# Decoder of twelve layers on one core: first operands of eight layers loaded while the layer ahead runs, and another order in two layers

## The chip, the cores and the metric

One core of a Trainium2 chip runs the whole kernel as one launch. The metric is the device time in microseconds (us), the median of several runs; lower is better. The engines have short names in the profile: PE is TensorE, DVE is VectorE, ACT is ScalarE, POOL is GpSimd, SP is the engine that only issues transfers (DMA).

## The reference

A pre-norm decoder of depth 4, three layers each time, over x (8 batches of 256 tokens, width 128, float32) and a context of 8 x 512 rows of width 96. `_layernorm` is taken in front of each layer, and the result is added to x.

```python
x = x + L0_attn(_layernorm(x), ...)            # 0  gated recurrence
x = x + L0_xattn(_layernorm(x), ctx_768, ...)  # 1  cross attention, 16 heads of 8
x = x + L0_ffn(_layernorm(x), ...)             # 2  mixture: 64 experts, top 8, all computed
x = x + L1_attn(_layernorm(x), ...)            # 3  self attention, 16 heads of 8
x = x + L1_xattn(_layernorm(x), ctx_768, ...)  # 4  cross attention, one head
x = x + L1_ffn(_layernorm(x), ...)             # 5  FP4-quantised MLP
x = x + L2_attn(_layernorm(x), ...)            # 6  causal attention, 16 heads of 64
x = x + L2_xattn(_layernorm(x), ctx_768, ...)  # 7  cross attention, one head, inner norms
x = x + L2_ffn(_layernorm(x), ...)             # 8  shared expert, top-1 expert on 256 tokens
x = x + L3_attn(_layernorm(x), ...)            # 9  latent attention with rope
x = x + L3_xattn(_layernorm(x), ctx_768, ...)  # 10 cross attention, 16 heads of 8
x = x + L3_ffn(_layernorm(x), ...)             # 11 sign-quantised linear
```

The two layers whose inner order changes:

```python
# L0_ffn, xf = x as 2048 x 128, 64 experts of width 64
aff = xf @ centroids.T
_, idx = jax.lax.top_k(aff + expert_biases, 8)
w = jax.nn.sigmoid(take_along_axis(aff, idx)); w = w / (sum(w) + 1e-8)
cw = zeros((T, E)).at[arange(T)[:, None], idx].add(w)
h = silu(einsum('td,edf->etf', xf, W_up)); y = einsum('etf,efd->etd', h, W_down)
out = silu(xf @ Ws_up) @ Ws_down + einsum('etd,te->td', y, cw)

# L2_ffn, 256 tokens are picked by index_b, index_t
shared_out = _ln(silu(x1) * x2) @ sw3 + sb3
out_all    = _ln(silu(h1) * h2) @ ew3 + eb3          # per expert, picked tokens
final_out  = shared_out.at[index_b, index_t].set(shared_w * shared_out[...] + expert_w * expert_out)
```

## The kernel before

x stays in SBUF for the whole kernel. Each layer is one function with a block of five programs, one per engine, written out by hand; engines meet through semaphores. `allocators` gives a layer its tiles and semaphores, and its `clear` ends the layer with a barrier of all engines (L166). So nothing of a layer, its transfers included, starts before every engine is through with the layer ahead: the layer's own SP program issues all of its loads. The functions are `layer_attention_heads8` (layers 1, 3, 10), `layer_attention_single` (4, 7), `layer_fp4_mlp` (5), `layer_attention_heads64` (6, 9), `layer_moe_top8` (2) and `layer_selected_experts` (8).

**Layer 2** (`layer_moe_top8`, names `L_ffn_...` between 454 and 723 us of the span). 2048 tokens go in four groups g of 512. A group has 33 steps: step j=0 is the shared expert, the others are 32 pairs of experts. In step n TensorE does `up(n)` into `psU`, ScalarE `silu(n)` into one of 20 `act` tiles, VectorE `weigh(n)` (times the pair's weights, L2110), and TensorE, `LAG` = 17 steps later, `down(n)`, which gathers in `psY`. The pair's weights must stand on 128 partitions, 64 for each expert (e=0, e=1): the routing weights `cw` are turned by TensorE (`turn_weights`), copied by ScalarE (`copy_weights`, `cwT`), written to DRAM (`weights_by_expert`, L2036) and read back as a broadcast into `cwb`, a chunk of four pairs at a time, two transfers of 512 KB each (L2044), four chunks deep. The routing of group g+1 runs inside group g: on VectorE `route_a` (copy of the affinities `aff`, top 8) and `route_b`, on ScalarE `sigmoids` with a table load before and after. For group 0 and 1 the places are these:

```python
                if n == 10:
                    turn_weights(0)
                if g + 1 < NG:
                    if j == 12:
                        turn(g + 1)
                    if j == 14:
                        affinities(g + 1)
                    if j == 26:
                        turn_weights(g + 1)
```

and VectorE has `weigh(n)` first, then `route_a(g + 1)` at j == 16. ScalarE has `sigmoids(g + 1)` at j == 19.

**Layer 8** (`layer_selected_experts`, `L_ffn_...` between 1497 and 1560 us). For each batch b of 256 tokens the shared expert is `project(b)` (`psX`, L2614), a gated unit on ScalarE and VectorE (`uT`), `out(b)` (`psT`, L2634), layer-norm statistics by `out_moments(b)` on VectorE, a root on POOL (`orr`), and `take(b)` on VectorE, which adds to x. The 256 picked tokens have units SEL, BIAS and TURN of their own; their results come as `value`, are split into three bfloat16 parts (`part`) and are put in place by `scatter(b)` on TensorE (a bias matmul, L2706, and twelve products with a 0/1 matrix `spread`, L2712), and `add(b)` on VectorE. `project(6)` uses the bank that TURN's result was in, so it waits for `x_read`, which came with `rw` (L2551).

## Time and profile before

| what | us |
|---|---|
| median of 3 runs | 2268.08 (2263.37 to 2271.72) |
| profiled execution, its own time | 2276.47 |
| its span | 2274.7 |
| mean granted clock of TensorE | 0.909 |

The span is divided by the layers' starts at about 3.6 (layer 0), 106.3 (1), 454.4 (2), 723.4 (3), 919.0 (4), 980.7 (5), 1077.9 (6), 1423.8 (7), 1497.0 (8), 1560.2 (9), 1936.6 (10) and 2236 (11). A row of the timeline has the start, the duration, the engine and line, output and inputs, and in brackets how long the engine was idle ahead of it and what ended that. SPq and POOLq are the queues of an engine that issues transfers; PEld is TensorE's load of the stationary operand. The granted clock (PEclk) is 1.00 for 2.4 GHz and 0.50 for 1.2 GHz.

### The profile page before, as it was taken

How to read it: one execution, taken by the hardware profiler on the slowest of the kernel's cores; microseconds unless marked ns; L12 is line 12 of the kernel's file. 1: busy time of each engine (PE TensorE's matmuls, PEld its weight loads, DVE VectorE, ACT ScalarE, POOL GpSimd, SP SyncE). 2: the span in 40 equal slices, each digit the busy share in tenths (PEclk: the TensorE clock that was granted, in tenths of full speed). 3: DMA queues.
4: the chain of work that ended last, by engine and by line, in shares of the span. 5: the costliest groups of instructions: out<-in, count | busy, mean ns of one | idle time of the engine just before them, and what ended most of it. 6: DMA issues, size and time to landing. Idle time of an engine off the chain costs nothing. (4 is left out here: it accounts for less than half of the span.)

```text
span 2274.7 us, 37358 instructions
## 1 busy us (share of the span) xinstructions
PE 1980.8 (87%) x12479; PEld 1178.8 (52%) x12479; DVE 1396.7 (61%) x3165; ACT 1115.1 (49%) x2823; POOL 657.7 (29%) x940
## 2 busy tenths in 40 slices
PE   6769999969997788856999999887999999699987
PEld 3424454424443455534666676565666666244444
DVE  5458889644542665478666666674656665567762
ACT  4325555534331476333555554341666666267762
POOL 7443432100002441300111110733443332533312
PEclk8859999979998799878999999896999999599996
DMA  1043131098661431100000000101000000443321
GB/s 35 17 93 92 47 85 43 2 202 174 149 145 30 98 86 31 32 10 7 33 1 1 1 1 2 32 23 49 1 2 1 2 1 2 110 97 86 73 44 27
DMA packets 120861, 111.90 MB, mean 49 GB/s; under 512 B 55862, under 2 KB 93410, under 8 KB 118370
## 3 DMA queue, kind: packets, MB, share of 16 engines
q1 hardware_dynamic: 87394, 108.47, 20.4%
q10 hardware_dynamic: 33280, 1.05, 0.7%
q8 instruction: 103, 1.69, 0.3%
q14 instruction: 84, 0.69, 0.1%
HBM read 93.30 MB, written 15.20 MB: 48 GB/s over the span
## 5 line engine op out<-in xcount | busy, mean ns | idle before, releaser
L997 DVE TENSOR_REDUCE L_xattn_mx<-L_xattn_psS 128x1 f32<-128x512 f32 x512 | 326.5, 684 | 124.2 <-PE L_xattn_psS L1124 119.9
L1234 ACT ACTIVATE L_xattn_PT<-L_xattn_psT 128x512 f32<-128x512 f32 x512 | 283.2, 600 | 95.4 <-PE L_xattn_psT L1136 89.7
L627 ACT ACTIVATE L_attn_pr<-L_attn_psS,L_attn_negm 128x256 f32<-128x256 f32 (+1 forms) x512 | 222.5, 447 | 52.0 <-PE L_attn_psS L538 33.6
L1124 PE MATMUL L_xattn_psS<-L_xattn_KR,L_xattn_QR 72*128 72x512 bf16 x512 | 213.0, 421 | 39.4 <-DMA L_xattn_QR<-L_xattn_q_parts 23.2
L407 DVE TENSOR_REDUCE L_attn_negm<-L_attn_psS 128x2 f32<-128x512 f32 x256 | 165.0, 686 | 116.3 <-PE L_attn_psS L528 116.2
L1136 PE MATMUL L_xattn_psT<-L_xattn_QR,L_xattn_KR 75*128 75x256 bf16 x1024 | 198.1, 278 | 3.9 <-ACT L_xattn_PT L1234 1.6
L1150 PE MATMUL L_xattn_psO<-L_xattn_PT,L_xattn_V 128*32 128x256 f32 x2048 | 188.9, 390 | 3.2 <-ACT L_xattn_PT L1234 1.1
L2110 DVE TENSOR_TENSOR L_ffn_act<-L_ffn_act,L_ffn_cwb 128x512 f32<-128x512 f32 x128 | 86.7, 691 | 129.6 <-ACT L_ffn_act L2240 105.9
L528 PE MATMUL L_attn_psS<-L_attn_qk 64*128 64x256 f32 x1024 | 146.1, 403 | 8.7 <-ACT L_attn_pr L627 8.5
L2175 PE MATMUL L_ffn_psU<-L_ffn_hT,L_ffn_wup 128*128 128x512 f32 x256 | 133.2, 611 | 13.8 <-ACT L_ffn_act L2240 13.8
L2240 ACT ACTIVATE L_ffn_act<-L_ffn_psU 128x512 f32<-128x512 f32 (+1 forms) x132 | 78.5, 597 | 135.2 <-PE L_ffn_psU L2175 131.3
L332 POOL TENSOR_TENSOR L_attn_qk<-L_attn_rotc,L_attn_rots 128x512 f32<-128x512 f32 x64 | 81.1, 1267 | 210.2 <-DVE L_attn_rotc L395 163.6
L1136 PEld LDWEIGHTS L_xattn_psT<-L_xattn_QR,L_xattn_KR 75*128 75x128 bf16 x1024 | 100.3, 100 | 77.4 <-issue 12.1
L337 POOL COPY L_attn_rinv<-L_attn_inv 128x256 f32<-128x256 f32 x128 | 50.9, 398 | 285.5 <-DVE L_attn_inv L420 285.5
L1150 PEld LDWEIGHTS L_xattn_psO<-L_xattn_PT,L_xattn_V 128*32 128x32 f32 x2048 | 89.1, 111 | 79.7 <-issue 22.8
L2188 PE MATMUL L_ffn_psY<-L_ffn_act,L_ffn_wdn 128*128 128x512 f32 x256 | 129.4, 598 | 1.1 <-DVE L_ffn_act L2110 1.1
L563 PE MATMUL L_attn_psOR<-L_attn_prT,L_attn_V 128*64 128x256 f32 (+1 forms) x1024 | 125.3, 365 | 5.7 <-ACT L_attn_spread L640 5.7
L548 PE MATMUL L_attn_psT<-ident,L_attn_pr 128*128 128x128 f32 x896 | 121.3, 275 | 0.0
L1124 PEld LDWEIGHTS L_xattn_psS<-L_xattn_KR,L_xattn_QR 72*128 72x128 bf16 x512 | 51.9, 102 | 133.4 <-DVE L_xattn_mx L997 75.9
L548 PEld LDWEIGHTS L_attn_psT<-ident,L_attn_pr 128*128 128x128 f32 x896 | 100.3, 141 | 38.4 <-issue 31.9
L640 ACT COPY L_attn_spread<-L_attn_psOR 128x256 f32<-128x256 f32 x128 | 47.8, 373 | 139.1 <-PE L_attn_psOR L570 139.1
L999 DVE TENSOR_REDUCE L_attn_mx<-L_attn_psS 128x2 f32<-128x512 f32 x128 | 84.4, 687 | 48.4 <-PE L_attn_psS L1124 47.7
(593 smaller groups left out, 3912.8 us busy)
## 6 DMA issues: line engine op xcount, KB each, us to landing
L_ffn_cwb<-L_ffn_weights_by_expert SPq DMA_DIRECT2D x64, 512.0 KB, 13.1
...
```

The lines of the kernel that those rows point to most:

```text
L407: nc.vector.tensor_reduce(negm[:, n % 4, :, r], psS[g % 3][:], AX.X, ALU.max, negate=True).then_inc(negm_ready, 1)
L528: ins = nc.tensor.matmul(psS[g % 3][:, t], qk[b % 2][at, j, 0, t * P:(t + 1) * P], qk[b % 2][at, j, 1], start=(t == 0 or not causal), stop ...
L548: ins = nc.tensor.transpose(psT[r][:, at:at + P], pr[n % 3][:, r, t, k * P:(k + 1) * P], m.ident[:])
L563: ins = nc.tensor.matmul(psOR[r * DH:(r + 1) * DH, 0, first:S], V[b % 2][:, k, hd * DH:(hd + 1) * DH], prT[n % 2][:, r, k * S:k * S + widt ...
L627: ins = nc.scalar.activation(pr[n % 3][:, r, t, 0:width], psS[(2 * n + r) % 3][:, t, 0:width], ACT.Exp, bias=negm[:, n % 4, t, r:r + 1], a ...
L997: nc.vector.reduce_max(mx[:, b % 2, u, hd:hd + 1], psS[n % 2][:], AX.X).then_inc(s_used, 1)
L1124: ins = nc.tensor.matmul(psS[n % 2][:, i * keys:(i + 1) * keys], QR[b % NB][0:PAIR, hd, t * P:(t + 1) * P], KR[b % NB][0:PAIR, hd, :], sta ...
L1136: ins = nc.tensor.matmul(psT[n % NPS][:, k], KR[b % NB][0:ROWS, hd, kt * P:(kt + 1) * P], QR[b % NB][0:ROWS, hd, :], start=True, stop=True)
L1150: ins = nc.tensor.matmul(psO[r:r + HW, g % 2], V[b % NV][:, kt, n % H], PT[n % NPT][:, kt], start=(kt == 0), stop=(kt == NKT - 1))
L1234: nc.scalar.activation(PT[n % NPT][:, 2 * u:2 * u + 2], psT[i % NPS][:], ACT.Exp).then_inc(exp_ready, 1)
L2175: ins = nc.tensor.matmul(psU[n % 2][:], wup[:, 2 * pair:2 * pair + 2].rearrange("p e f -> p (e f)"), hT[g % 2][:], start=True, stop=True)
L2188: ins = nc.tensor.matmul(psY[g % 2][:], wdn[:, pair], act_s[n % NA][:], start=False, stop=(pair == NP - 1))
```

## The change

1. Two regions of 128 x 1792 float32 live as long as the kernel. A table `AHEAD` says for layers 1, 4, 5, 6, 7, 8, 9 and 10 which of their loads go there; layer n uses region n % 2. At the end of its SP program each layer issues the loads of the next (`fetch_next`), and the next waits for them with `await_fetched` instead of for loads of its own.
2. In layer 2 the broadcast loads are split by half: SP issues e=0, POOL e=1. The weights of group 0 are turned at step 5, the routing of group 1 is moved forward in all four programs, and VectorE does it before its first `weigh`.
3. In layer 8 the folds of the constant matrices stand first, `out_moments(TURN)` comes earlier and itself releases `project(6)`, and the tail alternates `out(b)` and `scatter(b-1)`.

```diff
+    def fetch_next(self, sp):
+        n = LAYERS.index(self.at) + 1 if self.at is not None else 0
+        if n < len(LAYERS) and LAYERS[n] in AHEAD:
+            for dst, src in AHEAD[LAYERS[n]](self, self.region[LAYERS[n] % 2]):
+                sp.dma_start(dst, src).then_inc(self.fetched[LAYERS[n]], 16)
+
+    def await_fetched(self, eng, loads):
+        eng.wait_ge(self.fetched[self.at], 16 * loads)
...
+def fetch_heads8(m, region, pre, wk, wv):
+    ctx, wk_s, wqb, wv_s = heads8_ahead(region)
+    return [(ctx[0:DK], m.dram["ctx_768"][0]), (wk_s[0:DK], m.dram[wk]), (wqb, m.dram[f"{pre}_q_pack"]), (wv_s[0:DK], m.dram[wv])]
...
+def fetch_heads64(m, region, pre, causal):
+    half, down = heads64_ahead(region)
+    first = [(half.rearrange("p (i c) -> p i c", i=2), m.dram[f"{pre}_qk"][:, 0])]
+    return first if causal else [(down, m.dram["down_pack"])] + first
...
 # layer_attention_heads8, sync program
-            if from_ctx:
-                sp.dma_start(ctxT[:, 0], m.dram["ctx_768"][0]).then_inc(ctx_loaded[0], 16)
...
+            m.fetch_next(sp)
...
 # layer_moe_top8
+        def load_weights(queue, g, e, first=0, last=CHUNKS):
+            by_pair = c_dram[g % 2].rearrange("(n e) c -> e n c", e=2)
+            for i in range(first, last):
+                c = g * CHUNKS + i
+                wait(queue, weighted, CP * (c - NCH + 1))
+                src = by_pair[e:e + 1, i * CP:(i + 1) * CP].to_broadcast((F, CP, W))
+                queue.dma_start(cwb[c % NCH][e * F:(e + 1) * F], src).then_inc(cwb_loaded[e][c % NCH], 16)
...
+            root(0)
+            root(1)
+            for g in range(NG):
+                pool.wait_ge(cw_staged, 16 * (g + 1))
+                load_weights(pool, g, 1, 0, NCH)
+                if 1 <= g < NG - 1:
+                    root(g + 1)
+                load_weights(pool, g, 1, NCH, CHUNKS)
...
             normalise(1)
+            route_a(1)
+            route_b(1)
             for n in range(N + LAG + 4):
...
-                if n == 10:
-                    turn_weights(0)
-                if g + 1 < NG:
+                if n in (5, 18):
+                    turn_weights(n // 18)
+                if n == 9:
+                    turn(1)
+                if n == 11:
+                    affinities(1)
+                if 1 <= g < NG - 1:
...
 # layer_selected_experts, TensorE's tail and VectorE's
             out(2)
             project(6)
             scatter(0)
-            out(3)
             project(7)
             scatter(1)
-            out(4)
-            scatter(2)
...
+            for b in range(3, B):
+                out(b)
+                scatter(b - 1)
+            scatter(B - 1)
...
             for b in range(4, B):
-                add(b)
+                out_moments(b)
+                take(b - 1)
+                add(b - 2)
```

How it moves instructions, as the order of the programs shows it. First ScalarE in layer 2, groups 0 and 1, before (`L_ffn_act` are the silus, one per step; `L_ffn_sig` is the sigmoid of group 1):

```order
L2240 ACTIVATE L_ffn_act<-L_ffn_psU 64x512
L2240 ACTIVATE L_ffn_act<-L_ffn_psU 128x512 x10
L2234 COPY L_ffn_cwT<-L_ffn_psC 64x512
L2240 ACTIVATE L_ffn_act<-L_ffn_psU 128x512 x3
L2224 COPY L_ffn_hT<-L_ffn_psM 128x512
L2240 ACTIVATE L_ffn_act<-L_ffn_psU 128x512 x6
L2229 ACT_TABLE_LOAD
L2229 ACTIVATE L_ffn_sig<-L_ffn_aff 128x256
L2240 ACT_TABLE_LOAD
L2240 ACTIVATE L_ffn_act<-L_ffn_psU 128x512 x8
L2234 COPY L_ffn_cwT<-L_ffn_psC 64x512
```

and of the change:

```order
L2359 ACTIVATE L_ffn_act<-L_ffn_psU 64x512
L2359 ACTIVATE L_ffn_act<-L_ffn_psU 128x512 x5
L2353 COPY L_ffn_cwT<-L_ffn_psC 64x512
L2359 ACTIVATE L_ffn_act<-L_ffn_psU 128x512 x4
L2343 COPY L_ffn_hT<-L_ffn_psM 128x512
L2359 ACTIVATE L_ffn_act<-L_ffn_psU 128x512 x3
L2348 ACT_TABLE_LOAD
L2348 ACTIVATE L_ffn_sig<-L_ffn_aff 128x256
L2359 ACT_TABLE_LOAD
L2359 ACTIVATE L_ffn_act<-L_ffn_psU 128x512 x6
L2353 COPY L_ffn_cwT<-L_ffn_psC 64x512
```

The copy of the weights has moved from behind the tenth silu of 128 partitions to behind the fifth, and the sigmoid with its two table loads from behind the nineteenth to behind the twelfth.

POOL in layer 2, of the change (`L_ffn_rstd` are the roots of the four groups; before, POOL has these and no DMA):

```order
L2155 TENSOR_TENSOR L_ffn_veps<-L_ffn_moments,L_ffn_eps 128x4
L2157 TENSOR_TENSOR L_ffn_rstd<-L_ffn_veps,minus_half 128x4
L2155 TENSOR_TENSOR L_ffn_veps<-L_ffn_moments,L_ffn_eps 128x4
L2157 TENSOR_TENSOR L_ffn_rstd<-L_ffn_veps,minus_half 128x4
L2127 DMA L_ffn_cwb<-L_ffn_weights_by_expert 64x4x512 x12
L2155 TENSOR_TENSOR L_ffn_veps<-L_ffn_moments,L_ffn_eps 128x4
L2157 TENSOR_TENSOR L_ffn_rstd<-L_ffn_veps,minus_half 128x4
L2127 DMA L_ffn_cwb<-L_ffn_weights_by_expert 64x4x512 x8
L2155 TENSOR_TENSOR L_ffn_veps<-L_ffn_moments,L_ffn_eps 128x4
L2157 TENSOR_TENSOR L_ffn_rstd<-L_ffn_veps,minus_half 128x4
L2127 DMA L_ffn_cwb<-L_ffn_weights_by_expert 64x4x512 x12
```

All 32 halves e=1 stand now on POOL's queue; the root of group 2 stands behind the first twelve of them, that of group 3 behind twenty.

TensorE in the tail of layer 8, before (`psX` is a projection, `psT` an `out`, `part`x`spread` the scatter):

```order
L2614 MATMUL L_ffn_psX<-L_ffn_hT,L_ffn_wx 128x256
L2634 MATMUL L_ffn_psT<-L_ffn_w3i,L_ffn_uT 128x192 x2
L2614 MATMUL L_ffn_psX<-L_ffn_hT,L_ffn_wx 128x256
L2706 MATMUL L_ffn_psG<-L_ffn_b3p,L_ffn_ones 128x256
L2712 MATMUL L_ffn_psG<-L_ffn_part,L_ffn_spread 128x128 x12
L2634 MATMUL L_ffn_psT<-L_ffn_w3i,L_ffn_uT 128x192 x2
L2614 MATMUL L_ffn_psX<-L_ffn_hT,L_ffn_wx 128x256
L2706 MATMUL L_ffn_psE<-L_ffn_b3p,L_ffn_ones 128x256
L2712 MATMUL L_ffn_psE<-L_ffn_part,L_ffn_spread 128x128 x12
L2634 MATMUL L_ffn_psT<-L_ffn_w3i,L_ffn_uT 128x192 x2
L2706 MATMUL L_ffn_psC<-L_ffn_b3p,L_ffn_ones 128x256
L2712 MATMUL L_ffn_psC<-L_ffn_part,L_ffn_spread 128x128 x12
```

and of the change:

```order
L2718 MATMUL L_ffn_psX<-L_ffn_hT,region 128x256
L2738 MATMUL L_ffn_psT<-L_ffn_w3i,L_ffn_uT 128x192 x2
L2718 MATMUL L_ffn_psX<-L_ffn_hT,region 128x256
L2810 MATMUL L_ffn_psG<-L_ffn_b3p,L_ffn_ones 128x256
L2816 MATMUL L_ffn_psG<-L_ffn_part,L_ffn_spread 128x128 x12
L2718 MATMUL L_ffn_psX<-L_ffn_hT,region 128x256
L2810 MATMUL L_ffn_psE<-L_ffn_b3p,L_ffn_ones 128x256
L2816 MATMUL L_ffn_psE<-L_ffn_part,L_ffn_spread 128x128 x12
L2738 MATMUL L_ffn_psT<-L_ffn_w3i,L_ffn_uT 128x192 x2
L2810 MATMUL L_ffn_psC<-L_ffn_b3p,L_ffn_ones 128x256
L2816 MATMUL L_ffn_psC<-L_ffn_part,L_ffn_spread 128x128 x12
L2738 MATMUL L_ffn_psT<-L_ffn_w3i,L_ffn_uT 128x192 x2
```

`out(3)` has moved from in front of project(7) to behind scatter(1), and every later `out` now stands directly ahead of the scatter of the batch before it.

## Rows read from the trace of the kernel before

**Rows 1.** The page, part 1: busy time, share of the span, instructions
```profile
PE 1980.8 (87%) x12479; PEld 1178.8 (52%) x12479; DVE 1396.7 (61%) x3165; ACT 1115.1 (49%) x2823; POOL 657.7 (29%) x940
```

**Rows 2.** Windows in layer 2: us, busy by engine, PEclk, DMA share, GB/s
```profile
465.00:474.00 9.00, 9.00 (x19) 3.01 (x17) 4.16 (x18) 4.93 (x9) 1.21 (x2) 0.86 1.23 269
...
486.00:498.00 12.00, 6.25 (x14) 2.58 (x14) 6.13 (x11) 2.09 (x3) 0.00 (x0) 1.00 1.07 218
...
498.00:512.00 14.00, 5.24 (x7) 2.20 (x8) 11.34 (x33) 3.38 (x5) 0.00 (x0) 0.51 1.07 219
...
520.00:560.00 40.00, 40.00 (x102) 17.92 (x101) 17.06 (x34) 14.16 (x25) 1.56 (x2) 1.00 0.87 187
```

**Rows 3.** Timeline of layer 2, group 0: start us, us, instruction, idle before
```profile
476.15 0.51 SPq L2036 DMA_DIRECT2D L_ffn_weights_by_expert<-L_ffn_cwT  x1
...
485.86 2.50 DVE L2110 TENSOR_TENSOR L_ffn_act<-L_ffn_act,L_ffn_cwb 128x512 f32<-128x512 f32 x4 [15.09 <-DMA L_ffn_cwb<-L_ffn_weights_by_expert]
...
489.30 1.28 ACT L2229 ACT_TABLE_LOAD   x1
...
496.73 2.50 DVE L2110 TENSOR_TENSOR L_ffn_act<-L_ffn_act,L_ffn_cwb 128x512 f32<-128x512 f32 x4 [3.56 <-DMA L_ffn_cwb<-L_ffn_weights_by_expert]
...
501.52 2.50 DVE L2110 TENSOR_TENSOR L_ffn_act<-L_ffn_act,L_ffn_cwb 128x512 f32<-128x512 f32 x4 [2.29 <-DMA L_ffn_cwb<-L_ffn_weights_by_expert]
...
504.38 0.42 ACT L2229 ACTIVATE L_ffn_sig<-L_ffn_aff 128x256 f32<-128x256 f32 x1 [13.80 <-DVE L_ffn_aff L2083]
...
506.76 2.07 PE L2175 MATMUL L_ffn_psU<-L_ffn_hT,L_ffn_wup 128*128 128x512 f32 x2 [13.82 <-ACT L_ffn_act L2240]
...
511.98 1.02 PE L2188 MATMUL L_ffn_psY<-L_ffn_act,L_ffn_wdn 128*128 128x512 f32 x2
...
513.70 1.02 PE L2188 MATMUL L_ffn_psY<-L_ffn_act,L_ffn_wdn 128*128 128x512 f32 x2
```

**Rows 4.** Timeline, first waits of layers 1, 4, 5, 6, 7, 10
```profile
108.34 1.59 POOL L914 TENSOR_SCALAR L_xattn_h<-x,L_xattn_moments,L_xattn_rstd 128x128 f32<-128x128 f32 x2
...
110.01 2.05 PE L1097 MATMUL L_xattn_psS<-L_xattn_ctxT,L_xattn_wk 96*128 96x512 f32 x2 [5.36 <-DMA L_xattn_wq<-in_L_xattn_q_pack]
...
113.54 0.37 ACT L1187 COPY L_xattn_hT<-L_xattn_psT 128x256 f32<-128x256 f32 x1
...
921.73 0.74 PE L3046 MATMUL L_xattn_psO<-L_xattn_pack 128*128 128x97 f32 x2 [4.11 <-DMA L_xattn_pack<-in_L_xattn_pack]
...
986.31 1.32 DVE L1313 TENSOR_REDUCE L_ffn_bmax_w<-L_ffn_wall 128x70 f32<-128x1120 f32 x1 [1.36 <-DMA L_ffn_wall<-in_L_ffn_w_down]
...
1082.18 0.63 ACT L593 ACTIVATE L_attn_wqk<-L_attn_wqk 128x512 f32<-128x512 f32 x1 [2.78 <-DMA L_attn_wqk<-in_L_attn_qk]
...
1426.23 0.74 DVE L2977 BATCH_NORM_STATS2 L_xattn_cstats<-L_xattn_ctx 128x6 f32<-128x96 f32 x4 [1.64 <-DMA L_xattn_ctx<-in_ctx_rows]
...
1939.96 2.04 PE L1097 MATMUL L_xattn_psS<-L_xattn_ctxT,L_xattn_wk 96*128 96x512 f32 x2 [4.62 <-DMA L_xattn_wq<-in_L_xattn_q_pack]
```

**Rows 5.** Timeline, tail of layer 8
```profile
1531.71 0.92 PE L2634 MATMUL L_ffn_psT<-L_ffn_w3i,L_ffn_uT 64*128 64x192 f32 x4
...
1534.30 0.70 PE L2614 MATMUL L_ffn_psX<-L_ffn_hT,L_ffn_wx 128*128 128x256 f32 x2 [1.67 <-DVE L_ffn_rw L2551]
...
1547.17 1.46 PE L2712 MATMUL L_ffn_psE<-L_ffn_part,L_ffn_spread 128*128 128x128 bf16 x12
...
1548.56 1.65 PE L2634 MATMUL L_ffn_psT<-L_ffn_w3i,L_ffn_uT 64*128 64x192 f32 x4
...
1558.78 0.42 DVE L2452 TENSOR_TENSOR x<-x,L_ffn_psE 128x256 f32<-128x256 f32 x1 [1.29 <-PE L_ffn_psE L2712]
```

**Rows 6.** Windows at half clock: layer 8, layer 1, layer 10
```profile
1540.00:1555.00 15.00, 15.00 (x82) 11.04 (x81) 6.49 (x29) 0.47 (x1) 4.30 (x10) 0.50 0.00 0
...
109.00:167.00 58.00, 38.08 (x98) 15.73 (x100) 31.80 (x64) 13.49 (x24) 30.91 (x41) 0.50 0.46 102
...
1938.00:2000.00 62.00, 44.76 (x139) 18.77 (x140) 33.16 (x66) 16.38 (x33) 30.18 (x40) 0.51 0.46 110
```

More of the change, by code:

```diff
@@ L56, in __init__, with ahead @@
         self.half = self.sb("minus_half", [P, 64], F32)
+        self.region = [self.sb(f"region{i}", [P, AHEAD_COLS], F32) for i in range(2)]
+        self.fetched = {n: ctx.enter_context(nc.semaphore(f"fetched{n}")) for n in AHEAD}
+        self.at = None
+    def ahead(self):
+        return self.region[self.at % 2]
+    def fetch_next(self, sp):
[5 more added lines that the diff above has]
+        eng.wait_ge(self.fetched[self.at], 16 * loads)
     def sb(self, name, shape, dt=F32):
@@ L156, in pool_rsqrt, with carve, single_ahead, fetch_single @@
     return nc.gpsimd.tensor_tensor(w.rstd[:, 0:n], w.veps[:, 0:n], m.half[:, 0:n], ALU.pow)
+AHEAD_COLS = 1792
+def carve(region, *widths):
+    at = [sum(widths[:i]) for i in range(len(widths) + 1)]
+    return [region[:, a:b] for a, b in zip(at, at[1:])]
+def single_ahead(region):
+    return carve(region, 2 * D + 2 * (DK + 1) + 3, SK)
+def fetch_single(m, region, pre, inner_norm):
+    pack, first = single_ahead(region)
+    if inner_norm:
+        return [(first[:, 0:KT * DK].rearrange("p (t c) -> p t c", t=KT), m.dram["ctx_rows"][0].rearrange("(t p) c -> p t c", p=P)), (pack, m.dram[f"{pre}_pack"])]
+    return [(pack, m.dram[f"{pre}_pack"]), (first[0:DK], m.dram["ctx_768"][0])]
@@ new lines, in fp4_ahead, with fetch_fp4, experts_ahead @@
+def fp4_ahead(region):
+    return carve(region, 6 * D + 352)
+def fetch_fp4(m, region, pre):
+    wall, = fp4_ahead(region)
+    loads = []
+    for n, (c, k) in enumerate(((0, 128), (128, 128), (256, 96))):
+        loads.append((wall[0:k, n * D:(n + 1) * D], m.dram[f"{pre}_w_gate"][c:c + k]))
+        loads.append((wall[0:k, 3 * D + n * D:3 * D + (n + 1) * D], m.dram[f"{pre}_w_up"][c:c + k]))
+    return loads + [(wall[:, 6 * D:], m.dram[f"{pre}_w_down"])]
+def experts_ahead(region):
+    idx_row, idx_col, wx, cols, gates, cen, w3, ew3, e8, beta = carve(region, 512, 4, 137, 3, 17, P, D + 1, 4 * D, 2 * 64 + D, 32)
+    return (idx_row.bitcast(I32).rearrange("p (a m) -> p a m", a=2), idx_col.bitcast(I32).rearrange("p (a t) -> p a t", a=2), wx, cols, gates,
+            cen, w3[0:65], ew3.rearrange("p (n d) -> p n d", n=4), e8[0:8], beta.rearrange("p (n e) -> p n e", n=4))
@@ L217, in layer_attention_heads64 @@
         HALF = H * DH // 2
-        wqk, wv = sb("wqk", [P, 2, 2, HALF]), sb("wv", [P, H * DH])
+        first_half, down = heads64_ahead(m.ahead())
+        wqk = [first_half.rearrange("p (i c) -> p i c", i=2), sb("wqk", [P, 2, HALF])]
+        wv = sb("wv", [P, H * DH])
         wo = sb("wo", [P, NP, D])
@@ L283, in _, with await_half @@
                 sp.dma_start(bo[:], rows(d[f"{pre}_bo"]).to_broadcast((P, D))).then_inc(o_loaded, 16)
+            m.fetch_next(sp)
+        def await_half(eng, i):
+            if i == 0:
+                m.await_fetched(eng, 2 - causal)
+            else:
+                eng.wait_ge(half_loaded, 16)
         @block.gpsimd
@@ L493, in run @@
                     for i in range(2):
[L494 removed]
+                        ins = nc.tensor.matmul(banks[0][:, i], wqk[j // (NP // 2)][:, i, c], hT[b % 2][:], start=True, stop=True)
                     ins.then_inc(job_ready, 1)
@@ L724, in layer_attention_heads8 @@
         sb, ps, sem = allocators(nc, es, pre)
-        wqb, wk_s, wv_s, wo_s = sb("wq", [P, D + 2 * (bq is not None)]), sb("wk", [CK, D]), sb("wv", [CK, D]), sb("wo", [P, D])
+        if from_ctx:
+            ctx_first, wk_s, wqb, wv_s = heads8_ahead(m.ahead())
+            ctx_first, wk_s, wv_s = ctx_first[0:CK], wk_s[0:CK], wv_s[0:CK]
+        else:
+            wqb, wk_s, wv_s = sb("wq", [P, D]), sb("wk", [CK, D]), sb("wv", [CK, D])
+        wo_s = sb("wo", [P, D])
         wq_s = wqb[:, 0:D]
@@ L764, in layer_attention_heads8 @@
         block = es.enter_context(nc.Block())
-        WQK, WV = (2, 2) if bq is not None else (2, 1)
         SPLITS = 2
@@ L2049, in _, with root @@
             link(nc.gpsimd.memset(eps[:], LN_EPS))
-            for g in range(NG):
+            def root(g):
                 pool.wait_ge(moments_ready, g + 1)
@@ L2760, in _ @@
             scatter(0)
-            out(3)
             project(7)
             scatter(1)
-            out(4)
-            scatter(2)
-            out(5)
-            scatter(3)
-            out(6)
-            scatter(4)
-            out(7)
-            for b in range(5, B):
-                scatter(b)
+            for b in range(3, B):
+                out(b)
+                scatter(b - 1)
+            scatter(B - 1)
         @block.scalar
@@ L2799, in _ @@
             normalise(2)
+            act.wait_ge(fold_done, 1)
+            nc.scalar.copy(b3[:], psE[1][:, 0:D]).then_inc(fold_read, 1)
+            nc.scalar.copy(w3i[:, 0:D], psE[1][0:F, D:2 * D]).then_inc(fold_read, 1)
             read_turned(1)
@@ L2858, in layer_attention_single @@
         sb, ps, sem = allocators(nc, es, pre)
-        pack = sb("pack", [P, 2 * D + 2 * DA + 3])
+        pack, first = single_ahead(m.ahead())
         wqT, wkT, bq, wvT, wo = (pack[:, a:a + n] for a, n in ((0, D), (D, DA), (D + DA, 1), (D + DA + 1, DA), (D + 2 * DA + 1, D)))
@@ L2868, in layer_attention_single @@
         NCT = 3
-        ctxT = [sb(f"ctxT{i}", [DA, SK]) for i in range(NCT)]
+        ctxT = [sb(f"ctxT{i}", [DA, SK]) if i or inner_norm else first[0:DA] for i in range(NCT)]
         if inner_norm:
-            ctx = sb("ctx", [P, B, KT, DK])
+            ctx = [first[:, 0:KT * DK].rearrange("p (t c) -> p t c", t=KT) if b == 0 else sb(f"ctx{b}", [P, KT, DK]) for b in range(B)]
             cstats, cmom, ceps, crstd = sb("cstats", [P, B, KT, 6]), sb("cmom", [P, B, KT, 2]), sb("ceps", [P, B, KT]), sb("crstd", [P, B, KT])
```

240 lines of the change are left out of this document (115 added, 125 removed).

## The prediction

> **What bounds the kernel now.** I read the page first. TensorE is busy 1980.8 of 2274.7 us, the others between 29% and 61% [rows 1]. So the gain to be had is where TensorE stands still, or runs at half its clock, in the stretches that the diff touches. There are three kinds: the start of eight layers, the first token group of layer 2, and the last 25 us of layer 8. I then read windows and the timeline around each.
>
> In layer 2 the windows show the hole. TensorE is full from 465 to 474 (9.00 of 9.00) and again from 520 to 560 (40.00 of 40.00), but between 486 and 512 it works 6.25 + 5.24 of 26 us, and its granted clock is 0.51 from 498 to 512. The DMA share is 1.07 there: the 16 DMA engines are full with the broadcast weights `cwb` [rows 2]. The timeline gives the order of the waits [rows 3]. The staged weights leave at 476.15; VectorE's first `weigh` stands 15.09 us and begins at 485.86, when the first chunk is in. Behind its chunks stands the routing of group 1: ScalarE's sigmoid has waited 13.80 us for VectorE's copy of the affinities when it starts (504.38), and TensorE, whose `up` needs the silu behind that sigmoid in ScalarE's program, is idle 13.82 us until 506.76. So this is not the DMA bound that the share suggests. It is one sigmoid in a bad place: later groups show the same transfers (share 0.87) under a full TensorE [rows 2].
>
> At the starts of layers the timeline names a DMA as the last wait, with 1.4 to 5.4 us in front [rows 4]. In layer 8's tail the granted clock is 0.50 from 1540 to 1555 with TensorE full (15.00 of 15.00) [rows 6]: the four matmuls of `out` take 0.92 us before the fall and 1.65 after, the twelve of `scatter` 1.46, and the last addition to x begins at 1558.78 [rows 5].
>
> **Layer 2.** The cost of the change is worked out along the chain that opens `down`. Turning group 0's weights at step 5 would let the staging go some five steps of `up` earlier than 476.15, but SP's queue still holds the loads of `wdn`: the DMA share stays at 1.23 until 474 [rows 2]. I put the staging at 474, 2.2 us earlier, and by the present distance of 9.7 us (485.86 - 476.15) the first chunk at 483.6. Before TensorE gets there, ScalarE now does the sigmoid of group 1 at step 12, with a table load before and one behind: 1.28 + 0.42 + 1.28 = 3.0 us [rows 3]. VectorE has nothing else there, so the affinities don't wait. The silus between step 12 and `down(1)` come 3 us later than now; that and the turn of group 1's weights, which then stands in front of `down(1)`, put `down(1)` at about 488.5. Now it follows the first `weigh` (485.86 + 0.7), so it starts 1.9 us later than before, but without the hole behind it. From there `down` runs at the steady pace of 1.72 us (two matmul pairs, 1.02 us each, overlapped by 0.3; it is the step from 511.98 to 513.70, and the pace of 520 to 560). A chunk is four such steps, 6.9 us, and chunks land every 4.8 us now (VectorE's groups of four begin 4.8 us apart, 496.73 and 501.52), so none is late [rows 3]. The seventh `down` then comes at 488.5 + 6 x 1.72 = 498.8 instead of 513.70: 14.9 us. The turn of group 1's weights, about 0.6 us of TensorE, is done by then: **15.5 us**. The bounds: 17.8 if the two table loads hide under TensorE's own work, 5 if chunks come so late that half the hole stays and the clock falls with it. As TensorE has no idle time afterwards in the layer, what is gained here stays.
>
> The other half of the chunks is now issued by POOL, 32 transfers of 512 KB. No row shows POOL issuing a DMA. From below: SP takes 0.51 us to issue one [rows 3], which hides completely, since POOL's only other work in the layer is a root per group. From above: a POOL that takes over 6.9 us for one would set the pace of all 32 chunks. I take the value near the lower end, cost nothing, because POOL has 6.9 us per chunk, thirteen times what SP needs. POOL's root of groups 2 and 3 stands behind four chunks; it may come some us late, but its affinities are used eight steps later.
>
> The Trainium skill, "DMA: Bandwidth & Descriptors", section "Rules for kernel authors", speaks against this edit: two transfers to disjoint partition halves serialize, on one ring or two, and spreading DMAs over issuing engines only saves issue time. The share of 1.07 agrees; by that rule the split is worth nothing, and my sum gives it nothing either. The same page, section on the SWDGE path, fits 2.0 us + bytes/436e3 for a DMA from POOL; that would be an estimate of 3.2 us for 512 KB, under 6.9.
>
> **The first operands of eight layers** now lie in a lasting region when the layer starts; the SP program ahead issues them at its end, while other engines still finish. Hidden under that, they cost nothing; they are 1 to 10 transfers, and if a queue were still busy they would land as late as now. What is late next decides the gain, layer by layer [rows 4].
> - Layer 1: the K matmul waits 5.36 us for the last load and starts at 110.01, in front of the turn of h in TensorE's program; the turned h is copied at 113.54. POOL has h at 108.34 + 1.59 = 109.93. With K done before that, turn and copy end at about 110.7: 2.8 us. All of Q, staging and scores hang on it.
> - Layer 10, the same code: its wait is 4.62 instead of 5.36; I take 2.5.
> - Layer 5: 1.36 us of VectorE, whole: 1.4. Layer 7: 1.64, whole: 1.6. Layer 6: ScalarE's scaling waits 2.78, but the projection behind it also needs the turned h: about half, 1.5. Layer 4: TensorE's wait of 4.11 covers the barrier too; VectorE's chain is tied to it only through one addition, so 1.4 as its neighbours. Layer 9: nothing, its first matmul waits for VectorE's normalised rows and not for a load.
> Sum 2.8 + 2.5 + 1.4 + 1.6 + 1.5 + 1.4 = **11.2 us**. Bounds 0 (all the loads' waits give way to the statistics of x) and 17 (each wait whole, 5.36 + 4.62 + 1.36 + 1.64 + 2.78, and 1.4).
>
> **Layer 8.** Its start has the folds ahead of the first turn and the small loads already in: 0.5 us. In the middle, project(6) waited for `rw`, started at 1534.30 and so lay in front of nothing but idle time [rows 5]; now it is released by the statistics that stand well before. The value and its part come about 1.7 us earlier, since take(1) and the second half of the spread mask have moved behind them. In the tail TensorE's program goes out(b), scatter(b-1), and VectorE's follows it. At the slow clock a batch is 1.65 + 0.4 + 1.46 = 3.5 us of matmuls (`out`, then the bias and the twelve products of `scatter`), overlapped to 3.3. What was idle in front of the fall (TensorE waiting 1.67 us for `rw`) is mostly gone, so I take the clock to stay up. Then VectorE bounds: statistics 0.6, take 0.61, add 0.4, with gaps 2.2 us a batch, and the layer ends at 1533.7 + 7 x 2.2 + 1.5 = 1550.6 instead of 1559.2: 8.6. With the start, **9 us**. If the clock falls all the same, the tail is as long as now and only the 1.7 and part of the start are left: 2.
>
> **Sum.** 15.5 + 11.2 + 9 = 35.7 us. Against the profiled execution: 2276.5 - 35.7 = 2240.8. That run is 8.4 us above the median of the three timed ones, 2268.1, and the same sum against the median gives 2232.4. I predict 2232.
>
> **The rivals.**
> (a) Layer 8's tail stays at the slow clock. For it: the part chain of VectorE still keeps TensorE waiting in front of scatter(0). Against it: project(6) is no longer in that gap. Gain 28.7, time 2239. Chance 0.23.
> (b) Part of layer 2's hole stays, since the halves come late: two issuers share engines that are full (share 1.07), and VectorE must have both. Layer 2 gives 5, the sum is 25, time 2243. Against it: the ring is four chunks deep. Chance 0.13.
> (c) The loads ahead don't do what they say: layers wait for the statistics instead, and 11.2 becomes 2. Time 2241. For it: x is finished only at the barrier. Chance 0.10.
> (d) The other side: POOL's issue sets layer 2's pace. The price is 32 x (t - 6.9) us, t being POOL's time per transfer. The gain of 35.7 is used up at t = 8.0, and t = 10 would give 2232 + 99 = 2331. For it: nothing in the trace shows a POOL-issued DMA; against it: SP's 0.51. Chance 0.04.
> (e) Two long stretches behind the starts of layers 1 and 10 run at half clock, 58 and 62 us (0.50 and 0.51) [rows 6]. TensorE is busy there only 38.08 and 44.76 us. If the earlier start keeps one of them at full clock, some 10 us more are gained: 2222. Chance 0.08. The forecast itself: 0.42.
>
> **Range and chances.** Low: 2232 less 2.3 (layer 2's bound), 6 of layers' starts and (e) in part, 2213. High: 2232 + 6.7 (a) + 10.5 (b) + 4 for what the three runs differ by, 2253. Left out are (d) and sums of (b) with (c). A measurement of this kernel can tell about 0.5%, 11.3 us. All but (d) and the coincidence of three small rivals lie below 2256.8: faster 0.87, same 0.08, slower 0.05.
>
> **What would show it.** In the profile after: no idle time of TensorE over 3 us between layer 2's start and its second group, and a granted clock near 1.00 from 486 on; the sigmoid of group 1 in front of the first `weigh`. At the starts of layers 1 and 10 the K matmul ends before the turn of h. In layer 8, `out` at 0.92 us through the tail. Wrong would be: a wait on `cwb` in every group, matmuls of 1.65 us in the tail, or POOL as the releaser in layer 2.

## The result and the profile after

| kernel | median, us | runs | ratio to before (95%) |
|---|---|---|---|
| before | 2271.41 | 6 (2263.37 to 2279.86) | |
| the change | 2250.89 | 6 (2238.37 to 2253.80) | 0.9896 (0.9872 to 0.9920) |

The medians are 20.5 us apart, the ratio says 24 (0.0104 x 2271); the prediction said 35.7. Two executions in the experiments below, of 2819.84 and 3709.41 us, stand far apart from all others (2226 to 2283) and are in none of the ratios. The profiled execution of the change is the fastest of its six, 2238.4 us with a span of 2236.6; set against the profile of before it shows 38 us. So one pair of profiles shows more than the medians do. The page and the transfers:

```profile
PE 1970.5 (88%) x12479; PEld 1172.7 (52%) x12479; DVE 1396.3 (62%) x3165; ACT 1113.7 (50%) x2823; POOL 678.3 (30%) x972
...
q1 hardware_dynamic: 78690, 91.69, 16.8%
q0 software_dynamic: 4608, 16.78, 2.9%
```

TensorE's busy time has come down by 10.3 us with the same 12479 matmuls [rows 1], at a mean granted clock of 0.917 instead of 0.909; 16.78 MB are now moved by POOL's queue.

The table has the length of each layer, from its first instruction (transfers aside) to the next layer's, and for layer 11, which starts at 2240.8 in the profile of before, to its last addition to x. The third and fourth columns are two profiles of the same program, the second one taken with the experiments below.

| layer | before | the change | the change, second profile |
|---|---|---|---|
| 0 gated recurrence | 102.6 | 99.9 | 103.5 |
| 1 cross attention | 348.1 | 343.4 | 346.7 |
| 2 mixture | 269.0 | 253.4 | 253.8 |
| 3 self attention | 195.6 | 192.8 | 191.9 |
| 4 cross attention, one head | 61.7 | 60.2 | 60.3 |
| 5 FP4 MLP | 97.2 | 94.9 | 96.3 |
| 6 causal attention | 345.9 | 344.5 | 344.4 |
| 7 cross attention, one head | 73.2 | 71.5 | 71.5 |
| 8 selected experts | 63.2 | 59.7 | 66.5 |
| 9 latent attention | 376.3 | 376.1 | 376.1 |
| 10 cross attention | 304.3 | 302.3 | 312.9 |
| 11 sign linear | 31.2 | 31.2 | 31.2 |

Layers 0 and 3 have no edit, but their lengths differ by up to 3.6 and 3.7 us between these three profiles, in both directions, and by 6.8 and 6.4 over the thirteen that are read below. That is how far one profile can be trusted here, and layers 8 and 10 differ by 6.8 and 10.6 between two executions of the same program. Layer 2 doesn't: 253.4 and 253.8.

**Layer 2.** The timeline of group 0 after (add 7.4 us for the clock of before, since the layer starts that much earlier), with the windows:

```profile
464.37 0.51 SPq L2144 DMA_DIRECT2D L_ffn_weights_by_expert<-L_ffn_cwT  x1
...
468.52 2.77 POOL L2127 DMA_DIRECT2D L_ffn_cwb<-L_ffn_weights_by_expert  x4 [6.32 <-DMA L_ffn_weights_by_expert<-L_ffn_cwT]
...
473.07 0.42 ACT L2348 ACTIVATE L_ffn_sig<-L_ffn_aff 128x256 f32<-128x256 f32 x1
...
475.45 2.94 PE L2290 MATMUL L_ffn_psU<-L_ffn_hT,L_ffn_wup 128*128 128x512 f32 x6 [2.51 <-ACT L_ffn_act L2359]
...
476.33 2.50 DVE L2223 TENSOR_TENSOR L_ffn_act<-L_ffn_act,L_ffn_cwb 128x512 f32<-128x512 f32 x4 [1.00 <-DMA L_ffn_cwb<-L_ffn_weights_by_expert]
...
480.24 2.50 DVE L2223 TENSOR_TENSOR L_ffn_act<-L_ffn_act,L_ffn_cwb 128x512 f32<-128x512 f32 x4 [1.42 <-DMA L_ffn_cwb<-L_ffn_weights_by_expert]
...
480.77 1.02 PE L2303 MATMUL L_ffn_psY<-L_ffn_act,L_ffn_wdn 128*128 128x512 f32 x2
...
491.07 1.02 PE L2303 MATMUL L_ffn_psY<-L_ffn_act,L_ffn_wdn 128*128 128x512 f32 x2
```
```profile
480.00:490.00 10.00, 10.00 (x28) 4.64 (x27) 4.99 (x8) 3.89 (x7) 1.23 (x2) 1.00 1.04 289
490.00:500.00 10.00, 10.00 (x24) 4.37 (x23) 7.49 (x12) 3.28 (x7) 0.62 (x1) 1.00 1.06 257
500.00:540.00 40.00, 40.00 (x102) 17.64 (x101) 20.82 (x51) 13.77 (x24) 6.49 (x10) 1.00 0.81 203
```

The sigmoid of group 1 is at 473.07, in front of VectorE's first `weigh` (476.33); no wait of TensorE of 13.8 us is left. Behind the layer's start, where it waits 5.46 us for the first normalised rows in both kernels, its longest in this group is 2.51 us, behind the two table loads. `down(1)` is the row at 480.77, `down(7)` that at 491.07: 498.5 in the time of before, where the prediction had 498.8, and where [rows 3] have 513.70. The clock stays at 1.00 in these windows.

**Starts.** Layer 1, the rows that answer to the first three of [rows 4]:

```profile
103.83 1.10 PE L1199 MATMUL L_xattn_psS<-region 96*128 96x512 f32 x2 [1.83 <-PEq L255]
...
105.69 1.59 POOL L1011 TENSOR_SCALAR L_xattn_h<-x,L_xattn_moments,L_xattn_rstd 128x128 f32<-128x128 f32 x2
...
108.05 0.37 ACT L1289 COPY L_xattn_hT<-L_xattn_psT 128x256 f32<-128x256 f32 x1 [1.47 <-PE L_xattn_psT L1211]
```

The K matmul runs before h is there, at 1.10 instead of 2.05 us, and the copy of the turned h starts 4.4 us after the layer (103.64) instead of 7.2 (113.54 - 106.29).

**Layer 8, the tail:**

```profile
1503.98 0.61 DVE L2558 SCALAR_TENSOR_TENSOR x<-L_ffn_psT,L_ffn_orr,x 128x128 f32<-128x128 f32 x2 [0.92 <-POOL L_ffn_orr L2486]
...
1504.65 1.28 PE L2738 MATMUL L_ffn_psT<-L_ffn_w3i,L_ffn_uT 64*128 64x192 f32 x4 [1.39 <-DVE x L2558]
...
1507.57 1.65 PE L2738 MATMUL L_ffn_psT<-L_ffn_w3i,L_ffn_uT 64*128 64x192 f32 x4
```
```profile
1503.00:1504.60 1.60, 0.26 (x5) 0.08 (x2) 0.69 (x4) 0.00 (x0) 0.87 (x2) 1.00 0.00 0
1504.60:1521.00 16.40, 16.35 (x86) 11.90 (x86) 8.36 (x42) 0.00 (x0) 5.60 (x12) 0.51 0.00 0
```

TensorE waits 1.39 us for take(1), the clock falls 0.4 us behind the end of that wait (1505.06), and from the next one on `out` takes 1.65 us, as before [rows 5].

### The profile page after: what moved, and what is told of

Its sections match the earlier page's. It is cut to its first block and busy times, and to the rows that moved or that the text cites. A ratio compares the mean times of both kernels' runs of the same rounds, so it can differ in the third digit from the quotient of the medians.

```text
span 2236.6 us, 37360 instructions
## 1 busy us (share of the span) xinstructions
PE 1970.5 (88%) x12479; PEld 1172.7 (52%) x12479; DVE 1396.3 (62%) x3165; ACT 1113.7 (50%) x2823; POOL 678.3 (30%) x972
## 3 DMA queue, kind: packets, MB, share of 16 engines
q1 hardware_dynamic: 78690, 91.69, 16.8%
q0 software_dynamic: 4608, 16.78, 2.9%
## 5 line engine op out<-in xcount | busy, mean ns | idle before, releaser
L1336 ACT ACTIVATE L_xattn_PT<-L_xattn_psT 128x512 f32<-128x512 f32 x512 | 283.2, 600 | 95.4 <-PE L_xattn_psT L1238 89.6
L1252 PE MATMUL L_xattn_psO<-L_xattn_PT,L_xattn_V 128*32 128x256 f32 x2048 | 191.9, 397 | 3.2 <-ACT L_xattn_PT L1336 1.1
```

The costliest lines, as they stand in the source:

```text
L1252: ins = nc.tensor.matmul(psO[r:r + HW, g % 2], V[b % NV][:, kt, n % H], PT[n % NPT][:, kt], start=(kt == 0), stop=(kt == NKT - 1))
L1336: nc.scalar.activation(PT[n % NPT][:, 2 * u:2 * u + 2], psT[i % NPS][:], ACT.Exp).then_inc(exp_ready, 1)
```

## Experiments

All are edits of the changed kernel, except the one that says so. Each was timed in turn with the kernel before, in three groups of four, each group on another chip; the ratio is to that. The kernel before had medians of 2276.23, 2273.77 and 2268.82 us in the three groups, so kernels of different groups are compared by their ratios and not by their medians.

**The change again.** No edit.

> The changed kernel itself once more, to have a second profile and a ratio beside the three that follow. Theory A (the profile of the change is typical, the layers sum to 32 us of gain in the touched layers): ratio to before 0.985 to 0.987, and layers 0 and 3, which the change does not touch, take 99.9 and 192.8 us again. Theory B (the profiled execution was a lucky one): ratio 0.990 to 0.992, layers 0 and 3 back near 102.6 and 195.6 us, and the gain of layer 2 (15.6 us) stays in the profile.

Median 2250.17, ratio 0.9884 (0.9852 to 0.9915), between the two theories and the same as the first. Layers 0 and 3 took 103.5 and 191.9: neither "back" nor "again", they vary by themselves. The span was 2261.9, 25 us more than the first profile's, and 17 of these are in layers 8 and 10. Windows in the middle and tail of layer 8:

```profile
1496.00:1512.00 16.00, 16.00 (x48) 11.55 (x48) 8.17 (x31) 1.32 (x3) 2.84 (x6) 0.50 0.00 0
1512.00:1519.00 7.00, 5.71 (x42) 3.83 (x41) 4.37 (x15) 1.41 (x3) 1.65 (x2) 0.94 0.02 4
1519.00:1537.00 18.00, 17.74 (x98) 13.16 (x98) 9.50 (x45) 0.00 (x0) 5.60 (x12) 0.52 0.00 0
```

The clock is at 0.50 in the middle of the layer too (the first row), where the first profile has 1.00. Over the thirteen profiles of this study, in either order of layer 8, such a stretch is 17 to 21 us long in four, 3 to 7 us in six, and missing in three, before and the first of the change among these. Where it is long the layer takes 4.5 us more (59.3 against 54.8, take(1) first) to 6.8 us more (66.5 against 59.7, the change). So 38 was a lucky pair, and theory B is right in that.

**Loads at the layer's own start.**

```diff
     def fetch_next(self, sp):
-        n = LAYERS.index(self.at) + 1 if self.at is not None else 0
...
+        pass
+
+    def fetch_own(self, sp):
+        n = self.at
+        if n in AHEAD:
+            for dst, src in AHEAD[n](self, self.region[n % 2]):
+                sp.dma_start(dst, src).then_inc(self.fetched[n], 16)
...
 # first statement of each layer's SP program
+            m.fetch_own(sp)
```

> The changed kernel with part 1 undone: the same regions and waits, but each layer's own SP program issues its loads at its start. Theory A (loads ahead save what the first waits showed, 11 us over seven layers): 11 us above the changed kernel (ratio to before about 0.005 higher), the first waits on a DMA of 1.4 to 5.4 us back in layers 1, 4, 5, 6, 7, 10. Theory B (the starts wait for the statistics of x anyway): within 3 us of the changed kernel.

Median 2264.15, ratio 0.9949 (0.9932 to 0.9966), 0.0065 above the change, which is 15 us, with some 8 us to either side by the two intervals. The waits are back; TensorE at the start of layer 1:

```profile
105.34 2.04 PE L1204 MATMUL L_xattn_psS<-region 96*128 96x512 f32 x2 [5.89 <-DMA region<-in_L_xattn_Wv]
...
108.87 0.37 ACT L1294 COPY L_xattn_hT<-L_xattn_psT 128x256 f32<-128x256 f32 x1
```

Theory A. By layers, the means over ten profiles with loads ahead against three without (this one, before, and the new layer 2 alone): layer 1 344.7 and 347.8, layer 4 60.2 and 61.7, layer 5 95.4 and 96.4, layer 6 344.1 and 345.7, layer 7 71.6 and 73.5, layer 9 376.1 and 376.4. That is 9.3 us. Layer 10 has 303.6 and 307.7, of which the turned h alone accounts for 2.5 to 2.75 (4.42 or 4.17 us after the start instead of 6.92).

**Layer 2 as before.** The function of layer 2 is that of the kernel before, the rest of the change stays.

> The changed kernel with layer 2 as it was before. Theory A (the sigmoid of group 1 behind VectorE's chunks made the hole): layer 2 takes 269 us instead of 253.4, the kernel 15 to 16 us more than the changed one, ratio to before 0.007 higher. Theory B (the timed executions do not have this hole, and the 20 us of the medians come from elsewhere): less than 8 us above the changed kernel.

Median 2261.07, ratio 0.9944 (0.9924 to 0.9965), 0.006 above the change: 14 us; layer 2 takes 268.8. Theory A. The function goes back as a whole here. The split alone is tried further down; the earlier turn of group 0's weights and the earlier routing of group 1 were not timed apart. Of the two, the first can have brought about 2 us: the first chunk is used at 483.7 in the time of before instead of 485.86.

**The new layer 2 alone**, in the kernel before.

> The kernel before with the new layer 2 and nothing else. Theory A (layer 2's gain is independent of the rest): layer 2 takes 253.4 us, and the whole is 15.5 us under the kernel before, ratio 0.993. Theory B (part of it is lost again, by slow stretches of the clock that come elsewhere): ratio above 0.996 with layer 2 still at 253.4 us in the profile.

Median 2256.35, ratio 0.9930 (0.9911 to 0.9949), layer 2 at 253.1. Theory A: 16 us.

**Layer 8 in its order of before.** Its programs are in their order of before (folds late, `project(6)` released by `rw`, `out(3)` in front of `project(7)`); its loads still come ahead.

> The changed kernel with layer 8 in its order of before (its small loads still come ahead). Theory A (the new order is worth what the profile shows, 3.5 us less what the loads ahead give there, 0.7): 2 to 3 us above the changed kernel, the clock falls in the tail in either order. Theory B (the order is worth nothing, as the clock falls and TensorE's work at the slow clock sets the tail): within 1 us of it.

Median 2245.50, ratio 0.9869 (0.9851 to 0.9888). The median is 4.7 us under that of the change, by ratio 3, with intervals that overlap. Neither theory foresaw a lower median; what stands is that the new order gains nothing that can be measured. Its profile has layer 8 at 66.2 us, with a slow stretch of 6.8 us in the middle and the tail at half clock for its last 22.4 us.

**Who issues the halves: the split alone.** Layer 2 in its order of before, but halves e=1 on POOL's queue:

```diff
-                    for e in range(2):
-                        src = by_pair[e:e + 1, i * CP:(i + 1) * CP].to_broadcast((F, CP, W))
-                        sp.dma_start(cwb[c % NCH][e * F:(e + 1) * F], src).then_inc(cwb_loaded[c % NCH], 16)
+                load_weights(sp, g, 0)
...
+                load_weights(pool, g, 1, 0, NCH)
```

> The changed kernel with layer 2 in its order of before, but with the halves e=1 issued by POOL. Theory A (the split changes nothing, both halves share the same 16 engines): layer 2 takes 268.8 to 269.1 us as in the kernel before, chunks land 4.8 us apart. Theory B (the split makes the loads faster, 3.9 us a chunk as the changed kernel's first two): the hole is four chunks long, so layer 2 takes about 266 us.

Median 2256.97, ratio 0.9923 (0.9906 to 0.9940). VectorE's first chunk and its fourth:

```profile
481.21 2.50 DVE L2223 TENSOR_TENSOR L_ffn_act<-L_ffn_act,L_ffn_cwb 128x512 f32<-128x512 f32 x4 [13.80 <-issue]
...
495.67 2.50 DVE L2223 TENSOR_TENSOR L_ffn_act<-L_ffn_act,L_ffn_cwb 128x512 f32<-128x512 f32 x4 [2.58 <-DMA L_ffn_cwb<-L_ffn_weights_by_expert]
```
```profile
478.00:486.00 8.00, 6.92 (x16) 2.45 (x16) 3.50 (x6) 3.61 (x5) 0.62 (x1) 1.00 1.03 264
486.00:500.00 14.00, 2.29 (x6) 0.75 (x4) 8.22 (x21) 1.44 (x2) 1.85 (x3) 0.73 1.05 276
```

The layer starts at 451.09, so the first chunk is used after 30.1 us and the fourth after 44.6; with SP alone it was 31.4 and 47.1 [rows 3]. Layer 2 takes 266.6 instead of 268.8. Theory B in kind, 2.3 us in size: the halves on two queues move 264 to 276 GB/s where SP's alone moved 218 [rows 2], with the same share of the engines.

**Both halves on SP**, in the new order.

```diff
-                load_weights(sp, g, 0)
+                load_weights(sp, g, 0, 0, CHUNKS, both=True)
```

> The changed kernel, but SP issues both halves of the broadcast weights in layer 2 and POOL issues no transfer. Theory A (a chunk lands every 4.8 us when SP issues both halves, TensorE needs one every 6.9 us): layer 2 stays at 253.4 to 254.5 us, no difference in the whole. Theory B (POOL's half is part of the gain, since the changed kernel moves 257 to 289 GB/s in the same stretch where the kernel before moved 218): layer 2 takes 2 us or more longer, with a wait of VectorE on the weights in front of TensorE's second and third chunk.

Median 2246.74, ratio 0.9884 (0.9868 to 0.9899), the same as the change in the first group. Theory A, as far as the times tell: the profiled execution is the one of 2819.84 us, so nothing is read from it. The same edit with take(1) first, further down, has a profile of the usual length.

**take(1) first.** VectorE's program in the tail of layer 8:

```diff
                 link.mark(nc.vector.tensor_scalar(rest[:, t], rest[:, t], wt[:, t:t + 1], None, ALU.mult))
+            out_moments(1)
             n = r_at(TURN)
...
             gate_units(5)
-            out_moments(1)
             gate_units(6)
-            spread_part(1, 1)
             take(1)
             out_moments(2)
             gate_units(7)
+            spread_part(1, 1)
             add(0)
```

> The changed kernel with three of VectorE's steps in the tail of layer 8 moved: the statistics of out(1) in front of the value, take(1) directly behind it, the second half of the spread mask behind the next statistics. It takes away TensorE's wait of 1.4 us for take(1), behind which the granted clock fell in both profiles of the changed kernel. Theory A (that wait is what lets the clock fall): out stays at 0.92 us through the tail and layer 8 ends 7 to 8 us earlier, at about 52 us from its start when the middle of the layer isn't slow. Theory B (the clock falls for what came in front of it, the wait for the value included): the tail keeps 1.65 us per out and batches of 3.3 us, layer 8 gains 1 us at most.

Median 2235.99, ratio 0.9839 (0.9814 to 0.9864). Windows in the tail and one `out`:

```profile
1503.00:1506.00 3.00, 2.61 (x17) 1.43 (x16) 2.53 (x10) 0.36 (x1) 0.22 (x1) 0.68 0.02 5
1506.00:1509.00 3.00, 3.00 (x28) 2.46 (x27) 2.66 (x10) 0.11 (x1) 1.25 (x1) 0.75 0.00 0
1509.00:1512.00 3.00, 2.75 (x26) 2.07 (x23) 1.68 (x8) 0.00 (x0) 1.87 (x4) 1.00 0.00 0
1512.00:1520.00 8.00, 6.01 (x62) 4.29 (x60) 5.57 (x25) 0.00 (x0) 2.80 (x6) 1.00 0.00 0
```
```profile
1515.61 0.91 PE L2738 MATMUL L_ffn_psT<-L_ffn_w3i,L_ffn_uT 64*128 64x192 f32 x4 [0.24 <-DVE x L2558]
```

Layer 8 takes 54.0 us. Theory A in kind, but the layer is 5.7 us shorter than in the change's first profile and not 7 to 8, and the clock does fall, for 3.4 us from 1504.07 on, and comes back. From 1509 on it is at 1.00, a batch takes 2.15 us (1515.61 is the last of four at that distance), and the layer ends where the prediction had it: 63.2 - 9 = 54.2.

**take(1) first, once more.**

> The kernel with take(1) first once more, for a second profile and beside the next two on one chip. Theory A (the tail is fast every time): ratio 0.981 to 0.986, out at 0.92 us in the tail. Theory B (the first profile was a lucky one): ratio 0.987 to 0.990 and a tail at 1.65 us.

Median 2238.86, ratio 0.9861 (0.9838 to 0.9885). `out` at 0.91 to 0.92 in the whole tail, layer 8 at 54.8. Theory A on the profile; the ratio is at the upper end of it.

**Work added.** The changed kernel, in which scatter(1) is done twice:

```diff
-                nc.tensor.matmul(scatter_bank(b)[:, 0:TB * D], ones[:], b3p[:].rearrange("p t d -> p (t d)"), start=True, stop=False)
-                for i in batch(b):
+                for again in range(1 + (b == 1)):
+                    nc.tensor.matmul(scatter_bank(b)[:, 0:TB * D], ones[:], b3p[:].rearrange("p t d -> p (t d)"), start=True, stop=False)
+                    for i in batch(b):
```

> The changed kernel with work added and no step moved: TensorE does the thirteen matmuls of scatter(1) twice, the second time over the first, in the 1.4 us in which it otherwise waits for take(1). The result is the same. Theory A (TensorE standing still there is what lets the clock fall in the tail): with 1.1 us of matmuls more, the tail runs at 0.92 us per out in the profile, layer 8 gets 5 to 6 us shorter and the kernel comes down by about as much. Theory B (it was the order of the steps in the kernel with take(1) first that made the difference, not the idle time): the tail stays at 1.65 us per out and layer 8 is 0 to 1 us longer than in the changed kernel.

Median 2241.16 (2239.52 without the execution of 3709.41 us), ratio 0.9853 (0.9826 to 0.9881). The place of the wait and the tail:

```profile
1513.41 0.84 PE L2817 MATMUL L_ffn_psE<-L_ffn_part,L_ffn_spread 128*128 128x128 bf16 x12
...
1514.65 0.92 PE L2738 MATMUL L_ffn_psT<-L_ffn_w3i,L_ffn_uT 64*128 64x192 f32 x4 [0.40 <-DVE x L2558]
...
1517.02 0.91 PE L2738 MATMUL L_ffn_psT<-L_ffn_w3i,L_ffn_uT 64*128 64x192 f32 x4 [0.47 <-DVE x L2558]
```
```profile
1513.00:1514.60 1.60, 1.25 (x18) 0.85 (x15) 0.69 (x4) 0.00 (x0) 0.87 (x2) 1.00 0.00 0
1514.60:1526.00 11.40, 9.93 (x91) 7.29 (x92) 8.37 (x41) 0.00 (x0) 5.15 (x12) 1.00 0.00 0
```

The wait for take(1) is 0.40 us now instead of 1.39, TensorE is busy 1.25 of 1.60 us there and not 0.26, nothing else has changed place, and the tail runs at full clock: `out` 0.92 us, a batch 2.1 to 2.4. Layer 8 takes 61.2 us in this profile, with the slow stretch in its middle, where the change's second profile, with the same stretch, has 66.5. Theory A: 5.4 us from thirteen matmuls that compute nothing new, by these two profiles. The ratio is 0.003 to 0.004 under the two of the change, 7 to 10 us, but the intervals overlap, so the times alone don't show it.

The other profiles say the same. In all five profiles of kernels with this wait (the change twice, the loads at the layer's own start, layer 2 as before, the split alone) it is 1.38 or 1.39 us, and the clock falls 0.3 to 1.3 us behind it and stays down for 17 us or more. In the three profiles with the old order of layer 8 it falls within 3 us behind the wait of 1.66 or 1.67 us for `rw`. In the five in which the wait is closed (four by order, this one by work) the tail is at full clock until its last half microsecond, but for the 3.4 us above.

**Filler in the middle of layer 8**, on top of take(1) first:

```diff
             fold_bias()
+            pe.wait_ge(logits_ready, 1)
+            for _ in range(4):
+                nc.tensor.transpose(psC[:, 0:P], m.ident[:], m.ident[:])
             pe.wait_ge(oh_ready, 1)
```

> The kernel with take(1) first, and four turns of the identity into a free bank in front of TensorE's wait of 0.82 us for the choice of the expert in the middle of layer 8, after which the clock fell for 5 to 15 us in some profiles. Theory A (that wait is what lets the clock fall there): layer 8 at 54 us in the profile, and the median 3 to 5 us under the kernel without the four matmuls, since some of its executions have the slow stretch. Theory B (the fall has other grounds): within 2 us of it.

Median 2238.84 against 2238.86. Theory B: the slow stretch is in its profile (layer 8 at 59.3), though TensorE no longer stands still there. The wait of 0.82 us isn't what brings it.

**take(1) first, both halves on SP.**

> The kernel with take(1) first, and both halves of layer 2's broadcast weights issued by SP. Theory A (chunks land 4.8 to 5 us apart either way where the ring is full, and TensorE needs one every 6.9 us): layer 2 takes 253.4 to 254 us, the whole within 2 us of the kernel with POOL's halves. Theory B (POOL's half is part of the gain): layer 2 at 255.5 us or more.

Median 2238.87 against 2238.86; layer 2 at 253.8 against 253.3 and 253.4. Theory A.

## Why the prediction came out as it did

The time lies in the range, 2 us under its upper end, and the sign is right; the size is off: 24 us by the ratio where the sum had 35.7. That it is in the range is luck in part. The range had room for rival (a), which happened, and for rival (b), which didn't, and the second is what takes in the rest: the median of the kernel before rose from 2268.1 to 2271.4 with three more runs, and layer 8's order gave less than even (a) left it. Term by term:

- **Layer 2, 15.5.** Right, in mechanism and size: 15.6 in the first profile, 15.2 in the second, 14 and 16 us by the timed kernels without it and with it alone. The chain comes out within 0.4 us (first chunk 483.7 against 483.6 in the time of before, `down(1)` 488.2 against 488.5, `down(7)` 498.5 against 498.8). The first of these has luck in it, as two misses cancel: the staging left at 471.8 in that time and not at 474, so `wdn` held it up less than I took, and the first chunk was used 12.0 us later (476.33 - 464.37) and not 9.7. Rivals (b) and (d) are out: POOL is busy some 0.7 us with each transfer (2.77 for four), a tenth of the 6.9 it has.
- **"By that rule the split is worth nothing."** Taken so in the sum, and nothing is what it is worth in the new order: both pairs agree. But the reason is another than the rule's (the Trainium skill, "DMA: Bandwidth & Descriptors", section "Rules for kernel authors": two transfers to disjoint halves serialize). Two queues did move more, by a fifth or more; TensorE had no use for it, since a chunk every 4.8 us is enough for a need of 6.9. Where chunks were short, in the old order, it was worth 2.3 us.
- **Starts, 11.2.** Right: 2.8 predicted for layer 1 and 2.84 read at the turned h (3.1 over profiles); 2.5 predicted for layer 10 and 2.5 to 2.75 read; 1.4, 1.4, 1.5, 1.6 for layers 4, 5, 6 and 7, where the means over profiles give 1.5, 1.0, 1.6 and 1.9. The timed kernel gives 15 for all of them, layer 8's loads included. Rival (c) is out.
- **Layer 8, 9 us.** The step that failed is "What was idle in front of the fall (TensorE waiting 1.67 us for `rw`) is mostly gone, so I take the clock to stay up". Rival (a) happened. I had looked at the gap in front of scatter(0), where `project(6)` waited, and it was gone (TensorE waits 0.30 us for the part where it had waited 1.67 for `rw`). The change opened another one, 3 us later: take(1) and its statistics had moved behind the value, TensorE's `out(3)` needs the bank that take(1) frees, and there it waits 1.39 us. The kernels with that gap closed, by order or by idle work, run the tail at full clock but for 3.4 us in one profile, and with take(1) first the layer has the 54 us of the sum (54.0 and 54.8). The cost of the fall was sized at 7 us and measured at 5.4 and 5.7, so that is about right, and the fall itself was missed: a chain "what waits for the step that I move back" was not followed for take(1).
- **Rival (e)** did not happen: the stretch at 0.50 behind the start of layer 1 [rows 6] is 58.0 us long before, 54.6 in the first profile of the change and 58.0 in the second. The one of layer 10 is 61.4 us before and 54.6 in both. So the stretches stay, if anything a few us shorter.
- **What no term held:** the slow stretch in the middle of layer 8, and a second one in layer 10, that come in some executions of one program and not in others. They make 17 of the 25 us between its two profiles; its runs lie between 2238 and 2264. Summed by what the runs of the first group separate, 14 (layer 2) + 15 (loads, those of layer 8 among them) + (-3) (order of layer 8) = 26 us, against 24 and 26 measured for the whole. The pieces add up, more closely than intervals of some 8 us on each can promise. What brings the slow stretch in the middle of layer 8 is open: filling its most visible wait did nothing. The new order of layer 8 shortens the layer by 3.5 us in the first pair of profiles and gains nothing in the times; that it loses in the one stretch what it gains in the other is argued, not shown.

The best version that the experiments give is the change with take(1) first: 0.9839 and 0.9861. By ratio that is 5 to 13 us under the change (0.9884 and 0.9896), with which it was never timed in one group. In one group with it was the change with both halves on SP, which is as fast as the change elsewhere: 0.9884 against 0.9839, 10 us, with intervals that don't overlap.
